# Turns of expert tiles alone: one signal per tile load split into three, and transposes and first-layer products reordered

## The reference

```python
h = _L0_tok_ref(x, L0_tok_W, L0_tok_b)
h = jnp.concatenate([h, txt], axis=1)
h = h + _L0_attn_ref(_layernorm(h, axis=-1), L0_attn_Wq, L0_attn_Wk, L0_attn_Wv)
h = h + _L0_ffn_ref(_layernorm(h, axis=-1), ...)
...
top_vals, top_idx = jax.lax.top_k(logits, TOPK)
...
h = jax.nn.gelu(xn2 @ w1 + bb1, approximate=False)
return (acc + g[:, None] * (h @ w2 + bb2), None)
```

## Time and profile before

| | |
|---|---|
| median of three runs | 2925.34 us (2924.81 to 2934.8) |
| the profiled execution | 2913.08 us, span 2911.2 us |
| mean granted clock of the span | 0.892 |
| PE busy over the span | 2480.0 us, 85% |
| DVE, ACT, POOL busy | 1634.7, 1203.2, 785.4 us |
| DMA | 297.50 MB, mean 102 GB/s |

### The profile page before, as it was taken

The page is one execution under the profiler, slowest core; times in us unless marked ns, Lnnn a source line. Parts: engine busy times, 40 slices in busy tenths (PEclk is TensorE's granted clock), DMA queues, the critical chain, the costliest instruction groups (busy, mean ns, idle before and its releaser), DMA issues.

```text
span 2911.2 us, 62705 instructions
## 1 busy us (share of the span) xinstructions
PE 2480.0 (85%) x19692; PEld 1930.7 (66%) x19692; DVE 1634.7 (56%) x3896; ACT 1203.2 (41%) x2270; POOL 785.4 (27%) x1003
## 2 busy tenths in 40 slices
PE   3888999999999998999999999999976788888600
PEld 3856666666666666777777777777756777777500
DVE  2358778887877877666666666666642111111133
ACT  2223343344334333565666666566652323333200
POOL 1113223323333332222222222222211121211265
PEclk9669789898989988999999999999999989889855
DMA  6513112211311224244444444444333666766533
GB/s 117 143 18 46 28 28 44 41 28 33 52 28 28 48 37 113 63 115 114 113 105 105 105 105 105 108 107 110 96 110 124 217 225 211 232 208 208 162 110 96
DMA packets 267172, 297.50 MB, mean 102 GB/s; under 512 B 36156, under 2 KB 235304, under 8 KB 267112
## 3 DMA queue, kind: packets, MB, share of 16 engines
q1 hardware_dynamic: 248680, 264.80, 36.4%
q0 software_dynamic: 18432, 31.93, 3.8%
HBM read 236.04 MB, written 60.55 MB: 102 GB/s over the span
## 4 chain that ended last, share of the span: by engine, by line
PE 72%; issue 7%; DVE 7%; DMA 5%; POOL 3%; ACT 3%; SPq 2%; DVEq 0%; ACTq 0%; POOLq 0%
PE PS L1590 45%; PE PS L1734 7%; PE PS L1745 6%; DMA B2t<-in_L_ffn_b 4%; PE PS L1661 3%; PE PS L1711 3%; POOL pool L826 2%; DVE MX L1258 2%; PE PS L1784 1%; DVE rsi L1270 1%; PE PS L1622 1%; PE PS L1672 1%; ACT XE L988 1%; ACT pool L968 1%; DMA pool<-ybuf,ydst 1%
## 5 line engine op out<-in xcount | busy, mean ns | idle before, releaser
L1258 DVE TENSOR_REDUCE MX<-PS 108x2 f32<-108x648 f32 x576 | 460.6, 825 | 87.0 <-PE PS L1711 81.0
L968 ACT ACTIVATE pool<-PS 108x648 f32<-108x648 f32 x576 | 389.9, 711 | 217.1 <-PE PS L1734 178.6
L1590 PE MATMUL PS<-WB,big 128*128 128x192 f32 x2304 | 428.8, 343 | 2.6 <-ACT big L997 2.6
L1590 PE MATMUL PS<-XE,WF 128*128 128x256 f16 x2880 | 365.9, 281 | 56.9 <-ACT XE L988 46.6
L1590 PEld LDWEIGHTS PS<-WB,big 128*128 128x128 f32 x2304 | 397.9, 201 | 17.2 <-issue 10.0
L997 ACT ACTIVATE big<-PS,WF 128x256 f32<-128x256 f32 x576 | 241.5, 470 | 361.6 <-PE PS L1590 360.9
L1590 PEld LDWEIGHTS PS<-XE,WF 128*128 128x128 f16 x2880 | 277.2, 100 | 122.6 <-ACT big L997 40.8
L1402 DVE TENSOR_TENSOR big<-PS,B2t 128x384 f32<-128x384 f32 x96 | 53.5, 557 | 530.2 <-PE PS L1590 530.1
L826 POOL DMA_INDIRECT pool<-ybuf,ydst x192 | 193.7, 1009 | 481.7 <-DVE pool L1425 321.1
L814 POOL DMA_INDIRECT xbuf<-XH,DST x192 | 192.4, 1002 | 230.6 <-DVE DST L1340 169.1
L1270 DVE RECIPROCAL rsi<-rsi 128x324 f32<-128x324 f32 x96 | 209.1, 2178 | 3.3
(11 more groups left out here) (207 smaller groups left out, 4254.3 us busy)
## 6 DMA issues: line engine op xcount, KB each, us to landing
WF<-w1p SPq DMA_DIRECT2D x96, 771.0 KB, 4.7
WB<-in_L_ffn_W SPq DMA_DIRECT2D x96, 576.0 KB, 5.7
ximg<-in_x SPq DMA_DIRECT2D x96, 196.0 KB, 5.0
ximg<-in_x SPq DMA_DIRECT2D x96, 195.1 KB, 8.4
Xt<-xbuf SPq DMA_DIRECT2D x96, 192.0 KB, 2.5
ybuf<-big SPq DMA_DIRECT2D x96, 192.0 KB, 5.8
B2t<-in_L_ffn_b SPq DMA_DIRECT2D x96, 96.0 KB, 6.0
rbuf<-RP SPq DMA_DIRECT2D x32, 248.1 KB
```

The lines of the kernel that those rows point to most:

```text
L968: nc.scalar.activation(Pr[:, at:at + 2, :], pair(("st", p))[0:TP, :, 0:T], ACT.Exp, scale=SCALE2).then_inc(S["ex"], 1)
L1258: nc.vector.tensor_reduce(MX[:, qt, g, 64 * jj:64 * jj + 64:32], pair(("s", p))[0:TP, :, 0:T], AX.X, ALU.max).then_inc(S["mx"], 1)
L1590: last = nc.tensor.matmul(out_ap, lhsT, rhs, start=(i == 0), stop=(i == len(products) - 1))
```

## The change

The one counter of a tile's four DMAs is split in three: `rows` for the rows, `up` for the first layer's weights and bias, `down` for the second layer's weights and bias. `X` waits for `rows` alone, the first `W1` of a tile also for `up`, the first `W2` also for `down`. The order in which SP issues the DMAs is the same. This holds for the plans `BOTH` and `TILES`.

In the plan `TILES` alone the order of steps is changed. `X 1` now comes after the first unit of `W1 0` and not after the third; `X 2` comes before the second unit of `W1 1`, and so before `W2 0`; `X 0` (of the next turn) comes after the first unit of `W1 2`, before `W2 1`, where it stood after `W2 1` before.

```diff
 EXPERT = dict(
-    tin0=64, tin1=64, tin2=64, yo0=16, yo1=16, yo2=16,
+    rows0=16, rows1=16, rows2=16, up0=16, up1=16, up2=16, down0=32, down1=32, down2=32, yo0=16, yo1=16, yo2=16,
...
 TILE_STEPS = [
-    ("W1", 0, 0), ("ge", 0, 0), ("W1", 0, 1), ("ge", 0, 1), ("W1", 0, 2), ("ge", 0, 2), ("X", 1), ("xe", 1),
-    ("W1", 1, 0), ("ge", 1, 0), ("W2", 0, 0), ("W2", 0, 1), ("yv", 0), ("ld", 0), ("ys", 0), ("W1", 1, 1),
-    ("ge", 1, 1), ("W1", 1, 2), ("ge", 1, 2), ("X", 2), ("xe", 2), ("W1", 2, 0), ("ge", 2, 0), ("W1", 2, 1),
-    ("ge", 2, 1), ("W1", 2, 2), ("ge", 2, 2), ("W2", 1, 0), ("W2", 1, 1), ("yv", 1), ("ld", 1), ("ys", 1), ("X", 0),
-    ("xe", 0), ("W2", 2, 0), ("W2", 2, 1), ("yv", 2), ("ld", 2), ("ys", 2),
+    ("W1", 0, 0), ("ge", 0, 0), ("X", 1), ("xe", 1), ("W1", 0, 1), ("ge", 0, 1), ("W1", 0, 2), ("ge", 0, 2),
+    ("W1", 1, 0), ("ge", 1, 0), ("X", 2), ("xe", 2), ("W1", 1, 1), ("ge", 1, 1), ("W2", 0, 0), ("W2", 0, 1),
+    ("yv", 0), ("ld", 0), ("ys", 0), ("W1", 1, 2), ("ge", 1, 2), ("W1", 2, 0), ("ge", 2, 0), ("X", 0), ("xe", 0),
+    ("W1", 2, 1), ("ge", 2, 1), ("W1", 2, 2), ("ge", 2, 2), ("W2", 1, 0), ("W2", 1, 1), ("yv", 1), ("ld", 1),
+    ("ys", 1), ("W2", 2, 0), ("W2", 2, 1), ("yv", 2), ("ld", 2), ("ys", 2),
 ]
...
                 sp.dma_start(Xt[:, i, :, :], xbuf[bass.ds(row, TILE), :].rearrange("(s p) n -> p s n", p=128)
-                             ).then_inc(S[f"tin{i}"], 16)
+                             ).then_inc(S[f"rows{i}"], 16)
                 sp.dma_start(WF1[:, i, :], w1p[bass.ds(e, 1), :, :].rearrange("a p n -> (a p) n")
-                             ).then_inc(S[f"tin{i}"], 16)
+                             ).then_inc(S[f"up{i}"], 16)
                 sp.dma_start(WB2[:, i, :, :], w2[bass.ds(e, 1), :, :].rearrange("a (c p) n -> p (a c) n", p=128)
-                             ).then_inc(S[f"tin{i}"], 16)
-                sp.dma_start(B2t[:, i, :], b2[bass.ds(e, 1), :].to_broadcast([128, D])).then_inc(S[f"tin{i}"], 16)
+                             ).then_inc(S[f"down{i}"], 16)
+                sp.dma_start(B2t[:, i, :], b2[bass.ds(e, 1), :].to_broadcast([128, D])).then_inc(S[f"down{i}"], 16)
...
             def x_turn(turn, m, i):
-                pe.wait_ge(S[f"tin{i}"], due(f"tin{i}", m, 64))
+                pe.wait_ge(S[f"rows{i}"], due(f"rows{i}", m, 16))
...
             def w1_unit(turn, m, i, u):
                 if u == 0:
                     pe.wait_ge(S["x_evac"], due("x_evac", m, i + 1))
+                    pe.wait_ge(S[f"up{i}"], due(f"up{i}", m, 16))
...
             def w2_half(turn, m, i, s_):
                 if s_ == 0:
                     pe.wait_ge(S["gelu"], due("gelu", m, 3 * i + 3))
+                    pe.wait_ge(S[f"down{i}"], due(f"down{i}", m, 32))
```

More of the change, by code:

```diff
@@ L80 @@
 AHEAD = dict(
-    SP=("xin", "text", "keep", "tin0", "tin1", "tin2", "yo0", "yo1", "yo2", "rc0", "rc1", "out0", "out1"),
+    SP=("xin", "text", "keep", "rows0", "rows1", "rows2", "up0", "up1", "up2", "down0", "down1", "down2", "yo0", "yo1", "yo2", "rc0", "rc1", "out0", "out1"),
     PE=("emb", "tr1", "qk1", "v1", "s1", "p1t", "pv1", "tr2", "qk2", "v2", "s", "mt", "st", "pv", "pj", "tr3", "gate",
@@ L1367, in tables @@
                     for i in range(PER_TURN):
-                        dve.wait_ge(S[f"tin{i}"], due(f"tin{i}", GR * g - 1, 64))
+                        dve.wait_ge(S[f"down{i}"], due(f"down{i}", GR * g - 1, 32))
                     dve.wait_ge(pad_out, 16 * (E * g + 1))
```

## The result

The changed kernel took 2943.33 us (median of 21 runs), the kernel before 2934.36 in as many runs beside it: ratio 1.004, 95% interval [1.0027, 1.0052]. It is slower by 0.4%, where 1.2% had been forecast. The profiled execution has a span of 2920.9 us against 2911.2; both profiled executions are faster than the median of their kernel.

What follows compares the result with a forecast made beforehand. PE bounds attention with tiles; a chain through SP's loads bounds tiles alone. Group step 8.2, turn 16 to 17 0.7, 14 turns 29.7, less 5.0: 33.6 us on the 2925.3 median gives 2959, 8-in-10 range 2912 to 2990.

Steps and rivals of the forecast that it cites:

- The bound: Turns of tiles alone: a once-per-turn chain through SP's load and its landing, 30.44 us a turn, leaves PE idle.
- Split and X 1: Tile 1's transposes and first layer: no wait for rows or weights; old waits of 2.35 and 1.06 us gone.
- X 2: Tile 2's transposes, now before W2 0: start at yv1 + 11.83 us, PE idling 3.15 us for the rows.
- The estimate from the ring's order: Tile 2's rows land just behind load 1 and a store, at yv1 + 10.7; a turn 1.1 us shorter.
- SP sets it: Tile 2's rows: SP issues them only after load 1 and a store, at yv1 + 7.27, fixing when transposes start.
- X 0: Next turn's tile 0 transposes, before W2 1: start 5.08 us after W2 0 ends, PE idling 2.89 us.
- The chain at full clock: One turn from yv1 to yv1 without clock loss: 29.5 us, against 27.7 for the old chain.
- The clock: Behind both new waits PE's clock falls, costing 1.55 us each: 32.6 us a turn, 2.1 more than before.
- The rival with one fall a turn: Only one of the two waits lowers the clock: 31.1 us a turn, +10 us, 2935 us; chance 0.13.
- The step from group to group: Turn 15 to 16: tile 0's transposes precede work that ran during padding writes; yv1 of turn 16 comes 8.2 us later.
- The last turn: End of the tiles-alone stretch: no next tile 0 transposes, so 2.89 + 0.52 + 1.55 less, 5.0 us.
- The sum: Whole kernel: 8.2 + 0.7 + 29.7 less 5.0, 33.6 us slower; 2946.7 against the profiled execution, 2959 against the median.

## Why the prediction was wrong

- **The bound** was read rightly: in the turns of tiles alone it is a chain through SP's load, not PE; with the loads off the chain the turn fell to 22.8 us.
- **Split and X 1**: right. X 1 waits for nothing, W1 for its weights 1.3 us in fourteen turns.
- **X 2**: right in place. Forecast at yv1 + 11.83, measured +11.6 (issue +7.2, landing 4.3 in the mean). The estimate from the ring's order, a landing at +10.7, was the worse one: measured is +11.5. Nor was "SP sets it" the whole of it: with the issue 1.1 us sooner, X 2's rows were there only 0.5 us sooner.
- **X 0**: right. Forecast 5.08 us after the end of W2 0, measured 5.04 in the turn shown.
- **The chain at full clock**: 29.5 was forecast, 28.9 measured. The 34 and 44 records take 5.01 and 6.10 and not 5.17 and 6.26, and X 2 comes 0.2 sooner.
- **The clock**: this is the step that failed. "I take 1.55 for each, since work follows densely" was to be 3.1 us a turn; it measured 1.18 behind X 2 and 0.53 behind X 0, with the transposes 1.8. The price of one fall was nearly right, 1.67. Wrong was that every wait pays it. The argument, that all twelve waits before did, came from a wait with a copy's gap of 1.06 us right behind it: 2.35 idle, 0.5 of transposes and 1.06 idle again. The new waits are longer but single. 4.0 us of waiting always lowered the clock, 1.0 to 1.9 all but once kept it in the place of X 2, and between 2 and 3 us both happen. That the second gap made the difference is likely and not shown: no run has the old wait without it. The rival with one fall a turn (31.1 us, +10 us) came nearest, and by its count it was right, with 13 falls in 13 turns; its reason was not, as the falls are spread over both waits and some turns have two, some none.
- **The step from group to group**: right in size, and the hit in part luck. yv1 of turn 16 was forecast at 2296.8 and came at 2296.32, but turn 14 had ended 1.75 us sooner than before (2221.89 against 2223.64), so that the step itself is 9.5 us and not 8.2. Behind X 0 of turn 16 the clock cost 2.5 us (0.82 for 0.51, 8.31 for 6.10) and not 1.55. The last turn came out as worked out: 30.99 us from yv1 to the very last result, where the sum has 27.6 to the last yv1 and the trace shows 3.9 from there, 31.5.
- **The sum**: the forecast of 33.6 us was 8.2 for the step, 0.7 for turn 16 to 17, 27.6 for thirteen turns at 2.1, less 2.9 from there to the last result (one turn more at 2.1, less 5.0). Measured are 7.8, -0.6, 3.0 (399.03 us for thirteen turns against 396.07) and -3.5, and a tail 3.1 us longer, which had been set at nothing: 9.7 in all, and the medians differ by 9.0. The tail looks like chance, as the second trace of the changed kernel has 160.9 us there, the kernel before 160.2 and this one 163.3. Nearly all that is missing is in the thirteen turns, 24.6 us: 13 x 1.3 for the clock and 13 x 0.6 for the chain at full clock. What was gained beside the loss is the old turn's own 2.4 us of low clock and its copies' gaps: the new turn idles 5.7 us and loses 1.8, the old one idled 4.8 and lost 2.4.

What decides whether a wait pays is shown in two parts: its length (4.0 us always, under 2 us seldom), and for waits of 2.6 to 3.0 us where it ends in the time that the falls keep, whatever its place in the list. This would also account for much of the difference between the places: a turn of 30.7 us is about as long as the 30.72 us between falls, so that X 2 meets nearly the same moment turn after turn, and X 0 another that mostly spares it. What stays open is how much of X 2's 9 to 12 falls in 13 or 14 turns comes from its moments and how much from its waits, some of which are longer (up to 3.9 us): no run moves one without the other.

## What to carry to other kernels

Splitting a counter frees each consumer from the slowest load, here 2.3% by itself; moving the consumers earlier at the same time spends the gain, and more, when a step is put before the work that had covered its load. Set each step no earlier than trigger plus issue plus landing: here 5.1 us after its trigger for a free queue, and 11.6 after the first load's trigger for the second load in a row, against the work in between. With both transposes placed so the kernel was 2.7% faster than the one before on one chip and 3.8% on another. Count a wait's price as the wait and its clock, and take the chance of a fall from waits of the same length and shape: twelve falls out of twelve behind a wait with a second gap close to it did not carry over to single waits. A share counted at one turn length need not hold at another, since what counts is also the moment at which a wait ends.

## What the runs showed of the hardware

A low-clock stretch behind a single wait came mostly in one size: 1.67 us lost over 3.3 us (34 records in 6.68 for 5.01, 24 in 5.66 for 3.98, 44 in 7.77 for 6.10). After the 4 us waits it was more, 2.1 to 2.6 with the transposes slow as well. The Trainium skill, TensorE: Matmul & The Clock Gate, section HAM oscillation, has a DMA wait of 3 to 5 us in each pass of a loop lower the clock in every pass. The trace agrees for the waits of 4 us (13 turns of 13); of X 0's waits of 2.6 to 3.0 us, about the lower end of that, two thirds kept it (14 falls in 40 turns of three traces).

Where a low stretch begins is not set by the wait alone: in one trace eight in a row began 30.72 us apart, beside waits that ended 30.2 to 31.4 apart.

The rows of tile 1, whose load meets a free queue, landed in 2.2 to 2.6 us in every trace, while a turn went from 42 down to 22.8 us; those of tile 2, behind tile 1's load, took 3.1 to 6.0 where the trace shows their landing. Tile 0's rows took 2.4 to 2.6 us in the changed kernel and 3.1 to 4.6 in the turns of 22.8 us, where the core's DMA rate was 290 GB/s (2340 to 2600 us).
